# Router scores in four column groups, the first two experts' weights split during the attention, expert rows fetched by ScalarE

## What is computed

```python
# layer 0, attention: every second row, segments of 256 rows (128 used), 16 heads of 16
scores = einsum('bsqhd,bskhd->bshqk', qh, qh) * scale
seg_out = einsum('bshqk,bskhd->bsqhd', softmax(scores), qh)
# layer 0, feed-forward: one of 8 experts for each row
logits = x @ router_w + router_b
max_prob = max(softmax(logits)); max_ind = argmax(softmax(logits))
h = x @ w1[e]                      # 256 -> 2048, for the rows whose max_ind is e
a, g = split(h, 2)
y = silu(a) * g @ w2[e]            # 1024 -> 256
out = y * max_prob
# layer 1: linear attention, then a soft mixture over 64 x 32 slots
```

## Time and profile before

| | us |
|---|---|
| median of 3 executions | 1622.72 (1620.27 to 1627.33) |
| the profiled execution | 1626.27 |
| its span in the trace | 1624.2 |
| PE busy (matmul) | 1410.9 (87%) |
| VectorE, ScalarE, POOL busy | 948.4, 600.9, 665.6 |

### The profile page before, as it was taken

The page is one execution under the profiler, slowest core; times in us unless marked ns, Lnnn a source line. Parts: engine busy times, 40 slices in busy tenths (PEclk is TensorE's granted clock), DMA queues, the critical chain, the costliest instruction groups (busy, mean ns, idle before and its releaser), DMA issues. The chain is left out here.

```text
span 1624.2 us, 27351 instructions
## 1 busy us (share of the span) xinstructions
PE 1410.9 (87%) x8858; PEld 1214.0 (75%) x8859; DVE 948.4 (58%) x1810; ACT 600.9 (37%) x1007; POOL 665.6 (41%) x501
## 2 busy tenths in 40 slices
PE   6994626998998999379987999999999995999997
PEld 3442224887887888357767999999999975999997
DVE  4778451343334323336757878877877853556555
ACT  3443401222222222247654333333333314555553
POOL 6554146557357100431102756556655730440500
PEclk9996857999999999679998999999999997999999
DMA  4100415022222000530004235644553557455440
GB/s 152 56 26 5 177 51 156 14 90 90 87 90 90 13 13 17 176 110 1 1 1 130 79 93 154 181 122 137 168 169 98 159 142 285 143 195 191 164 158 31
DMA packets 109176, 171.15 MB, mean 105 GB/s; under 512 B 6112, under 2 KB 95072, under 8 KB 101696
## 3 DMA queue, kind: packets, MB, share of 16 engines
q1 hardware_dynamic: 100096, 156.00, 29.8%
q0 software_dynamic: 3408, 9.31, 1.9%
q10 hardware_dynamic: 5616, 5.11, 0.9%
HBM read 114.96 MB, written 55.44 MB: 105 GB/s over the span
## 5 line engine op out<-in xcount | busy, mean ns | idle before, releaser
L1448 PE MATMUL disp_psS<-disp_e,last_x 128*128 128x256 f32 x1024 | 233.1, 381 | 3.7 <-POOL disp_e L1531 3.7
L1448 PEld LDWEIGHTS disp_psS<-disp_e,last_x 128*128 128x128 f32 x1024 | 191.2, 191 | 28.4 <-POOL disp_e L1531 4.3
L1538 POOL TENSOR_TENSOR disp_s<-disp_e 128x512 f32<-128x512 f32 x64 | 82.4, 1287 | 262.9 <-ACT disp_e L1518 262.9
L1717 PE MATMUL comb_psO<-comb_yh,comb_eh 128*128 (+1 forms) x512 | 156.0, 305 | 15.0 <-DVE comb_el L1808 11.3
L1433 PE MATMUL disp_psL<-phi_hi,disp_xh 128*128 (+1 forms) x512 | 157.0, 307 | 4.9 <-DVE disp_e L1594 4.8
L1500 ACT ACTIVATE disp_raw<-disp_psL 128x512 f32<-128x512 f32 x128 | 76.5, 598 | 220.3 <-PE disp_psL L1433 155.6
L1531 POOL TENSOR_TENSOR disp_e<-disp_e,disp_rs 128x1024 f32<-128x1024 f32 x64 | 151.8, 2372 | 0.0
L1808 DVE TENSOR_TENSOR comb_el<-comb_psT,comb_eh 128x512 fp32r<-128x512 f32 x128 | 86.8, 687 | 105.0 <-ACT comb_eh L1753 105.0
L1433 PE MATMUL disp_psL<-phi_hi,disp_xl 128*128 (+1 forms) x512 | 145.6, 284 | 0.0
L1433 PE MATMUL disp_psL<-phi_lo,disp_xh 128*128 (+1 forms) x512 | 145.6, 284 | 0.0
L1717 PE MATMUL comb_psO<-comb_yl,comb_eh 128*128 (+1 forms) x512 | 145.0, 283 | 0.0
(11 more groups left out here) (258 smaller groups left out, 3542.7 us busy)
## 6 DMA issues: line engine op xcount, KB each, us to landing
logits<-disp_raw SPq DMA_DIRECT2D x64, 512.0 KB, 4.1
comb_e<-logits SPq DMA_DIRECT2D x32, 1024.0 KB, 4.9
w_raw<-in_w SPq DMA_DIRECT2D x8, 2048.0 KB
disp_wt<-in_w_slot SPq DMA_DIRECT2D x16, 1024.0 KB, 8.7
w_raw<-in_w SPq DMA_DIRECT2D x8, 1024.0 KB
disp_bt<-in_b_slot SPq DMA_DIRECT2D x8, 1024.0 KB, 11.3
comb_y_in<-slot_y SPq DMA_DIRECT2D x4, 2048.0 KB, 10.3
slot_y<-disp_yb SPq DMA_DIRECT2D x60, 128.0 KB, 2.8
```

The lines of the kernel that those rows point to most:

```text
L1448: last = nc.tensor.matmul(psS[kd][:, b, :], x[:, b * TB + mc, kd * P:(kd + 1) * P], e[mc % 4][:, b, :], start=mc == 0 and b % 2 == 0, stop ...
L1538: nc.gpsimd.tensor_tensor(s2[:], e[mc % 4][:, 0:2, :], e[mc % 4][:, 2:4, :], ALU.add).then_inc(pair_sum, 1)
L1717: last = nc.tensor.matmul(psO[j % 2][:, 0:D], ep[s % EB][:, i, :], yp[:, bass.ds(odd, 1), ch * D:(ch + 1) * D].rearrange("p a d -> p (a d) ...
```

## The change

The router's weights are padded with zeros to 32 columns, so that the scores of the four tiles of a group are made in four column groups of the array (8 matmuls of 128 columns in place of 2 of 512), and one transpose brings a group back. Experts 0 and 1 are split in the attention: in every second step ScalarE makes a sixteenth of the high parts of both (256 and 128 columns each), and after the masks of a segment POOL makes a sixteenth of the low parts. The raw weights of expert 1 lie where its low parts go. In the experts block the rows of a tile are copied by ScalarE at the end of the step before; POOL may split w1 of an expert once the last first product of the expert two before is done (`g_ready`), and PE waits for w1's two pieces ahead of the first product and for w2's ahead of the second.

```diff
@@ dilated_attention
-                    if not isinstance(i, int):
+                    if not isinstance(i, int) or i > 0:
...
             weights.load(sp, 0)
-            with sp.Fori(1, NSEG // 2) as i:
+            load(1, (2, 3))
+            weights.load(sp, 1)
+            with sp.Fori(2, NSEG // 2) as i:
...
                         ALU.mult).then_inc(xm_ready, 1)
+                    if g == UPS - 1:
+                        for e in range(2):
+                            seg = i * 2 + q - 2 - 2 * e
+                            if not isinstance(i, int) or seg >= 0:
+                                weights.low_slice(pool, e, seg)
...
                 masks(i)
+            for e in range(2):
+                for seg in range(NSEG - 2 - 2 * e, NSEG):
+                    weights.low_slice(pool, e, seg)
...
                     augment(*at, i + 1 + (k + 1) // 4)
+                for e in range(2):
+                    at = segment(i, k, 3 + 4 * e)
+                    if at is not None:
+                        weights.high_slice(act, e, at[0])
...
-            steps(act, step, 4)
+            steps(act, step, 8)
@@ normalise_and_route
+    EW = P // GT
...
-        logit_t = [m.sb(f"logit_t{i}", [NE, GT * P]) for i in range(2)]
-        rw = m.sb("rw", [P, KD, NE])
+        logit_t = [m.sb(f"logit_t{i}", [P, P]) for i in range(2)]
+        rw = m.sb("rw", [P, KD, EW])
...
-            weights.load(sp, 1)
...
-            weights.divide_low(pool, 0)
-            weights.divide_low(pool, 1)
+            nc.gpsimd.memset(rw[:], 0.0).then_inc(rw_clear, 1)
...
-                wait(pe, scores_ready, g - 1)
+                wait(pe, scores_ready, g)
                 for k in range(KD):
-                    last = nc.tensor.matmul(psL[g % 2][:], rw[:, k, :], xT[g % 2][:, k].rearrange("p a t -> p (a t)"),
-                                            start=k == 0, stop=k == KD - 1)
+                    for a in range(GT):
+                        last = nc.tensor.matmul(psL[a * EW:(a + 1) * EW, :], rw[:, k, :], xT[g % 2][:, k, a, :],
+                                                start=k == 0, stop=k == KD - 1, skip_group_check=True)
...
-                for a in range(GT):
-                    last = nc.tensor.transpose(psR[:, g * GT + a, :], logit_t[g % 2][:, a * P:(a + 1) * P], c["ident"][0:NE, 0:NE])
-                last.then_inc(routed, 1)
+                nc.tensor.transpose(psR[:, g * GT:(g + 1) * GT, :].rearrange("p t e -> p (t e)"), logit_t[g % 2][:],
+                                    c["ident"][:]).then_inc(routed, 1)
...
-            weights.divide_high(act, 0)
...
-            weights.divide_high(act, 1)
@@ Weights
+        self.next1 = m.over("next1", [P, KD, 2 * FF], lo1_at + 4 * KD * 2 * FF)
+        self.next2 = m.over("next2", [P, FK, D], lo2_at + 4 * FK * D)
...
+        raw1, raw2 = (self.next1, self.next2) if e == 1 else (self.raw1, self.raw2)
+        if e == 1:
+            sp.wait_ge(self.loaded1, 16)
+            sp.wait_ge(self.loaded2, 16)
+        else:
+            wait(sp, self.split, 4 * e)
...
+    def slices(self, e, seg):
+
+        raws = (self.next1, self.next2) if e == 1 else (self.raw1, self.raw2)
+        for (loaded, raw, hi, lo), source in zip(self.parts(), raws):
+            n = KD * 2 * FF // NSEG if raw is self.raw1 else FK * D // NSEG
...
+    def high_slice(self, act, e, seg):
+
+        for loaded, raw, hi, _ in self.slices(e, seg):
+            act.wait_ge(loaded, 16 * (e + 1))
+            last = self.nc.scalar.activation(hi, raw, ACT.Copy)
+        last.then_inc(self.high[e], 1)
+
+    def low_slice(self, pool, e, seg):
+
+        pool.wait_ge(self.high[e], seg + 1)
+        for _, raw, hi, lo in self.slices(e, seg):
+            last = self.nc.gpsimd.tensor_tensor(lo, raw, hi.bitcast(F32), ALU.subtract)
+        if isinstance(seg, int) and seg == NSEG - 1:
+            last.then_inc(self.split, 4)
...
-    def divide(self, pool, e):
+    def divide(self, pool, e, free):
...
+            pool.wait_ge(done, tiles)
@@ experts
-                pool.wait_ge(yo_ready, w_free)
-                w.divide(pool, e)
+                w.divide(pool, e, ((g_ready, w_free), (yo_ready, w_free)))
...
-                    pe.wait_ge(w.split, e * 4 + 4)
+                    pe.wait_ge(w.split, e * 4 + 2)
...
+                    e = pe.value_load(route["expert"][0:1, bass.ds(t, 1)], min_val=0, max_val=NE - 1)
                     b = buffer_of(t)
+                    pe.wait_ge(w.split, e * 4 + 4)
...
+            def fetch(t, q):
+                act.wait_ge(gathered[q], before(t, q, 4) + 16)
+                wait(act, x_turned, t)
+                nc.scalar.activation(xs[:], xg[:, bass.ds(t, 1), :].rearrange("p a d -> p (a d)"), ACT.Copy).then_inc(xs_ready, 1)
...
+                t = s + 1
+                if live(t):
+                    fetch(t, (q + 1) % 4)
+
+            fetch(0, 0)
...
-                    dve.wait_ge(gathered[q], before(t, q, 4) + 16)
-                    wait(dve, x_turned, t)
-                    v.tensor_copy(xs[:], xg[:, bass.ds(t, 1), :].rearrange("p a d -> p (a d)")).then_inc(xs_ready, 1)
```

More of the change, by code:

```diff
@@ L74, in sb, with over @@
         return self.ctx.enter_context(self.nc.sbuf_tensor(f"{self.tag}_{name}", shape, dt))
+    def over(self, name, shape, offset):
+        return self.nc.alloc_sbuf_tensor_at(f"{self.tag}_{name}", shape, F32, offset=offset)
     def ps(self, name, shape, dt=F32):
@@ L237, in masks @@
                         ALU.mult).then_inc(xm_ready, 1)
+                    if g == UPS - 1:
[3 more added lines that the diff above has]
+                                weights.low_slice(pool, e, seg)
             fill_constants(nc, c, pool)
             masks(0)
-            with pool.Fori(1, NSEG // 2) as i:
+            masks(1)
+            with pool.Fori(2, NSEG // 2) as i:
                 masks(i)
+            for e in range(2):
+                for seg in range(NSEG - 2 - 2 * e, NSEG):
+                    weights.low_slice(pool, e, seg)
         @block.tensor
@@ L532, in normalise_and_route @@
         psX = [m.ps(f"psX{i}", [P, 2, KD, P]) for i in range(XB)]
-        psL = [m.ps(f"psL{i}", [NE, GT * P]) for i in range(2)]
-        psR = m.ps("psR", [P, NT, NE])
+        psL = m.ps("psL", [P, P])
+        psR = m.ps("psR", [P, NT, EW])
         psAB = m.ps("psAB", [P, 2, NT, NE])
@@ L537, in normalise_and_route @@
         psI = m.ps("psI", [P, 2 * NCOL])
+        rw_clear = m.sem("rw_clear")
         (w_loaded, chain, kept, turned, xT_ready, scored, scores_ready, routed, diff_ready, exp_ready,
@@ L545, in _ @@
         def _(sp):
[L546 removed]
+            sp.wait_ge(rw_clear, 1)
+            sp.dma_start(rw[:, :, 0:NE], router_w.rearrange("(k p) e -> p k e", p=P)).then_inc(w_loaded, 16)
             sp.dma_start(rb[:], router_b.partition_broadcast(P)).then_inc(w_loaded, 16)
[L548 removed]
             for b in range(B):
@@ L644, in _ @@
             dve.wait_ge(routed, NT // GT)
-            link(v.tensor_tensor(logit[:], psR[:], rb[:].unsqueeze(1).to_broadcast([P, NT, NE]), ALU.add))
+            link(v.tensor_tensor(logit[:], psR[:, :, 0:NE], rb[:].unsqueeze(1).to_broadcast([P, NT, NE]), ALU.add))
             link(v.tensor_reduce(best[:], logit[:], X, ALU.max))
@@ L733, in __init__ @@
         self.hi1 = m.sb("hi1", [P, 2, KD * 2 * FF], F32R)
+        lo1_at = nc.sbuf_base
         self.lo1 = m.sb("lo1", [P, 2, KD * 2 * FF], F32R)
         self.hi2 = m.sb("hi2", [P, 2, FK * D], F32R)
+        lo2_at = nc.sbuf_base
         self.lo2 = m.sb("lo2", [P, 2, FK * D], F32R)
+        self.next1 = m.over("next1", [P, KD, 2 * FF], lo1_at + 4 * KD * 2 * FF)
+        self.next2 = m.over("next2", [P, FK, D], lo2_at + 4 * FK * D)
         self.zero = m.sb("zero", [P, 1])
         self.loaded1, self.loaded2, self.zeroed = m.sem("loaded1"), m.sem("loaded2"), m.sem("zeroed")
-        self.split, self.high = m.sem("split"), m.sem("high")
+        self.split, self.high = m.sem("split"), [m.sem(f"high{e}") for e in range(2)]
@@ L742, in load @@
     def load(self, sp, e):
-        wait(sp, self.split, 4 * e)
-        sp.dma_start(self.raw1[:], self.w1_dram[e].rearrange("(k p) f -> p k f", p=P)).then_inc(self.loaded1, 16)
-        sp.dma_start(self.raw2[:], self.w2_dram[e].rearrange("(k p) d -> p k d", p=P)).then_inc(self.loaded2, 16)
+        raw1, raw2 = (self.next1, self.next2) if e == 1 else (self.raw1, self.raw2)
[4 more added lines that the diff above has]
+            wait(sp, self.split, 4 * e)
@@ L748, in parts @@
     def parts(self):
         return ((self.loaded1, self.raw1, self.hi1, self.lo1), (self.loaded2, self.raw2, self.hi2, self.lo2))
-    def divide_high(self, act, e):
-        for loaded, raw, hi, _ in self.parts():
-            act.wait_ge(loaded, 16 * (e + 1))
-            self.nc.scalar.activation(hi[:, e, :], raw[:].rearrange("p k f -> p (k f)"), ACT.Copy).then_inc(self.high, 1)
-    def divide_low(self, pool, e):
```

(9 more changed lines are left out.)

8 lines of the change are left out of this document (4 added, 4 removed).

## The result

| | us |
|---|---|
| changed kernel, median of 4 executions | 1571.49 (1570.8 to 1573.55) |
| kernel before, median of 4 | 1621.49 (1620.27 to 1627.33) |
| ratio | 0.969, 95% interval 0.966 to 0.971 |
| profiled executions, before and after | 1626.27 and 1570.80 (-55.5) |
| their spans | 1624.2 and 1569.1 (-55.1) |

What follows compares the result with a forecast made beforehand. VectorE's chain was taken to bound scores and tables, PE the experts, a ring of engines the attention. 2.7 - 23.9 - 12.4 - 27.5 = -61.1 took the median from 1622.7 to 1561.6 us; 8-in-10 range 1542 to 1588.

Steps and rivals of the forecast that it cites:

- Part 1: Attention: splitting slices added on ScalarE and POOL cost 0 inside the loop, +2.7 us at its end (bounds 0 and 5).
- The three idles: Attention loop: waits of ScalarE (1.81 us), POOL (3.69) and VectorE (0.72) per segment cover the slices, so 0 added.
- Part 2: Scores: column groups and no POOL splitting beside VectorE's norm take the stage from 46.3 to 22.4 us, -23.9.
- Part 3: Tables: running-sum adds no longer stand under POOL's splitting, 14.5 us for five adds becomes 2.1, -12.4.
- Part 4: Experts: PE's waits for row copy and low parts go, with the clock's fall behind them, -27.5 us (other end 0).
- The stall: Start of the experts' tile loop, under POOL's gathers: PE gets few instructions; taken as unchanged, 0, with 20 us at stake.
- My rival: Experts' loop start: the stall moves because the new code lies elsewhere, vanishing (1542) or starting earlier (1572); chance 0.12.
- Less room: Attention ring: three VectorE operations stand for a whole POOL slice each, up to 35 us, giving 1570 to 1597; chance 0.10.
- scores don't get faster: Scores: column groups run one after another (+9.8) or PE stays at 1.2 GHz (+13), giving 1572; chance 0.07.
- gaps stay: Experts: ScalarE's copy or w2 is late, so the -27.5 falls away, giving 1589; chance 0.06.
- The slower one: Attention: a ring without room, where slices and standing VectorE add 96 us, giving 1658; chance 0.03.

Runs made afterwards that it cites:

- the last kernel: Changed kernel with gathers spread in experts and linear attention, and POOL making expert 1's slices one segment earlier; chip D: 1614.6 us, ratio 0.994.
- chip C: Changed kernel and kernel before, both rerun unaltered on another chip: medians 1528.9 us (ratio 0.963) and 1588.5 us.

## Why the prediction was right, point by point

Forecast 1561.6, measured 1571.5; direction and range right. Of the 9.9 us, 5.6 are the sum (-61.1 against -55.5 between the profiled executions). The other 4.3 are the way from there to the medians: I took 3.6 us off, and it was 0.7 to be added (1571.5 against 1570.8).

- *Part 1, +2.7.* Measured +3.9 in the two spans at the result, with POOL's last slices as the end, as said. The attention of one kernel ends at two places about 1.5 us apart: 145.5 to 145.7 or 146.9 to 147.1 us in ten profiled executions with the slices (the last kernel aside), 143.3 to 144.8 in three without. The means are 146.3 and 144.3, +2.0. What decides between them stays open. The three idles that I named did cover the slices inside the loop; ScalarE kept 0.81 us and POOL 0.38. The last experiment shows how they are lost: by a wait of POOL ahead of the masks.
- *Part 2, -23.9.* Measured -24.4. The sum by PE's period held nearly: 1.7 us a group where 1.88 was forecast. I added lengths, and the entries overlap; so they did before, where a group is 3.38 us by its lengths and 3.17 by its starts (169.42 to 172.59). The run with the splitting back in the routing shows VectorE's share, the one with whole scores PE's (11.8 us).
- *Part 3, -12.4.* Measured -12.4.
- *Part 4, -27.5.* Without a stall the stage from first gather to last `yo` went from 415.2 to 389.2 us, -26.0: right in kind and nearly in size. The reasons were right in kind too; but they don't add up, which I had not said.
- *The stall, 0.* This is the step that failed: "Gathers and loop keep their places, so I leave this stall as it is, with 20 us at stake". It cost 3.9 us more than before in the experts (24.2 against 20.3), and with Part 4's 1.5 that makes the 5.4 us by which the experts missed. The gathers kept their place against the routing's end, but the stall need not start with the loop: it now starts ahead of tile 0. Why it starts earlier was not found; it also does so with the old splitting, and the runs with the old copy fell on a chip without stall. My rival had "start earlier (+10)", more than twice the 3.9, and the wrong condition (where the loop lies); that its 1572 is so near the measured 1571.5 is luck.
- *The rivals.* "Less room", "scores don't get faster" and "gaps stay" did not come. The slower one was not seen; the last kernel is slow by another wait.
- On chip C the sum comes out: the ratio 0.9625 and -60.9 us between the spans, where -61.1 was forecast with the stall taken as constant. Part of that is luck, for the stages differ and cancel: attention +0.7 (forecast +2.7), scores and tables -37.3 (-36.3), experts -26.0 (-27.5), linear attention and the rest +1.8 (0).
- *The forecast's own range, 1551 to 1573.* It does not follow from the bounds that it names: 0 and 5 for Part 1 and -4.6 and +13 for Part 2 give 1554 to 1577.

## What to carry to other kernels

When engines idle without a releaser while another engine has a long row of indirect DMAs in flight, shorten that row: issue as many as the next tiles need, and the rest between other work; shortening it cost nothing on the chip that didn't stall and won some 25 us on the one that did. Before filling an engine's idle time in a ring, look at what each new wait stands in front of: POOL's slices were free with the high part there in time, and cost 7.4 us a segment when they were asked for one segment too early. One kernel's times on two chips differ by 32 us, more than most of the effects sought; compare within one chip, and look for the stage in which the chips differ.

## What the runs showed of the hardware

- The kernel before took 1621.5 us on chip A, 1624.0 on D, and 1589.5 and 1588.5 on B and C. In the traces of the result and of chip C the difference lies in the two stages that start under gathers. Where they stall, ScalarE, VectorE and PE all do: `yo` waits 25.0 us in the experts, and in the linear attention of the changed kernel ScalarE waits 17.0 us for something outside its core's records, on chip C not at all. The waits of the stage (us in total, times, longest), at the result:

```profile
ACT lin_ke L1204 <- remote: 17.0, 2, 10.3
PEld lin_psK L1142 <- issue: 12.8, 2, 9.0
```

- The Trainium skill ("Runtime: NRT & Kernel Launch", "Instruction fetch mechanics") calls the cost of crossing a block of instructions "mostly hidden". The trace agrees on chip C (PE is busy for all of 229.6 to 250.0 us under the same gathers); at the result it is busy for 6.97 us of that stretch. That the fetch of instructions starves is a reading that fits an idle time without a releaser, and it is not shown. The traces do hold packets of a queue named "instruction" (here in the changed kernel at the result, 195 to 252 us, and on chip C, 193 to 250: packets, MB, share of 16 engines' time):

```profile
q8 instruction: 2, 0.03, 0.2%
```

```profile
q8 instruction: 4, 0.07, 0.5%
```

That is about 1 us for a packet in both, so those that are recorded are fewer under the stall and not slower. Whether they come late and cause it, or come seldom because little is executed, stays open.
- A group's scores took 0.64 us as 16 entries of 128 columns in four column groups, and 1.88 us as 4 entries of 512: the same 2048 columns in a third of the time, so column groups do run beside each other here (the granted clock is 1.00 in both).
